# The scan of a four-operator image kernel: neighbour rows from a second, shifted copy of the state, in tiles of 32 columns

## The reference

```python
def _cell(prev_col, cur_col, weight_ih, bias_ih, weight_hh, bias_hh):
    C = cur_col.shape[-1]
    pad = jnp.pad(prev_col, ((0, 0), (1, 1), (0, 0)))
    x = jnp.concatenate([pad[:, :-2], pad[:, 1:-1], pad[:, 2:]], axis=-1)
    i_vals = jnp.einsum('bhk,ok->bho', x, weight_ih) + bias_ih
    h_vals = jnp.einsum('bhc,oc->bho', cur_col, weight_hh) + bias_hh
    r_i, z_i, n_i = jnp.split(i_vals, 3, axis=-1)
    r_h, z_h, n_h = jnp.split(h_vals, 3, axis=-1)
    r = jax.nn.sigmoid(r_i + r_h)
    z = jax.nn.sigmoid(z_i + z_h)
    n = jnp.tanh(n_i + r * n_h)
    return n * z + cur_col * (1.0 - z)
```

## Time and profile before

| | |
|---|---|
| Time, median of 3 runs | 601.97 us (601.34 to 603.91) |
| Span of the profiled execution | 600.5 us |
| PE busy | 551.9 us (92%), 7884 instructions |
| PE weight loads busy | 460.9 us (77%) |
| DVE busy | 469.2 us (78%), 1272 instructions |
| ACT busy | 394.4 us (66%), 897 instructions |
| POOL busy | 300.7 us (50%), 425 instructions |
| The chain that ended last | PE 39%, DVE 34%, ACT 15%, issue 9% of the span |

### The profile page before, as it was taken

The page is one execution under the profiler, slowest core; times in us unless marked ns, Lnnn a source line. Parts: engine busy times, 40 slices in busy tenths (PEclk is TensorE's granted clock), DMA queues, the critical chain, the costliest instruction groups (busy, mean ns, idle before and its releaser), DMA issues.

```text
span 600.5 us, 21552 instructions
## 1 busy us (share of the span) xinstructions
PE 551.9 (92%) x7884; PEld 460.9 (77%) x7884; DVE 469.2 (78%) x1272; ACT 394.4 (66%) x897; POOL 300.7 (50%) x425
## 2 busy tenths in 40 slices
PE   3999999699999999999999999988889897999996
PEld 2333333599998989899999999988477776899995
DVE  7778977377777777777778777888899999477876
ACT  3445889766666666666667966775468986766441
POOL 7665653156565655555565122035789799221000
PEclk9999999899999999999999999999999998999999
DMA  6900000011111111111111300001237675003324
GB/s 224 384 2 0 2 2 4 14 38 39 39 41 37 44 35 44 35 44 35 44 35 43 125 1 1 0 1 51 92 117 239 217 245 171 33 1 141 140 123 158
DMA packets 21282, 45.66 MB, mean 76 GB/s; under 512 B 5104, under 2 KB 15600, under 8 KB 20352
## 3 DMA queue, kind: packets, MB, share of 16 engines
q1 hardware_dynamic: 20160, 44.97, 23.2%
q10 hardware_dynamic: 672, 0.15, 0.1%
q0 software_dynamic: 416, 0.07, 0.1%
HBM read 28.53 MB, written 8.39 MB: 61 GB/s over the span
## 4 chain that ended last, share of the span: by engine, by line
PE 39%; DVE 34%; ACT 15%; issue 9%; DVEq 2%; DMA 1%; SPq 0%; POOL 0%; ACTq 0%; POOLq 0%
PE psum L645 8%; DVE work L326 5%; PE psum L755 5%; PE psum L894 5%; PE psum L910 5%; DVE spec L1343 5%; ACT spec L1001 5%; DVE spec L1335 5%; ACT spec L1009 5%; DVE spec L1338 4%; PE psum L813 4%; DVE small L1221 3%; PE psum L771 3%; PE psum L883 2%; PE psum L739 2%
## 5 line engine op out<-in xcount | busy, mean ns | idle before, releaser
L684 PE MATMUL psum<-spec,matrices 128*64 128x128 f32 x2016 | 154.7, 275 | 2.3 <-issue 1.5
L680 PE MATMUL psum<-spec,matrices 128*64 128x128 f32 x1512 | 132.4, 282 | 6.3 <-DVE spec L1343 3.7
L684 PEld LDWEIGHTS psum<-spec,matrices 128*64 128x64 f32 x2016 | 119.8, 138 | 3.1 <-issue 1.7
L522 POOL TENSOR_TENSOR spec<-spec 32x120 f32<-32x120 f32 x126 | 59.8, 475 | 88.5 <-DVE spec L1338 88.5
L680 PEld LDWEIGHTS psum<-spec,matrices 128*64 128x64 f32 x1512 | 85.3, 137 | 20.4 <-DVE spec L1343 8.6
L645 PE MATMUL psum<-spec,matrices 128*64 128x512 f32 x384 | 86.7, 609 | 1.0 <-ACT spec L935 1.0
L813 PE MATMUL psum<-work 128*32 128x128 f32 x2368 | 74.3, 278 | 14.0 <-ACT work L338 11.3
L813 PEld LDWEIGHTS psum<-work 128*32 128x32 f32 x2368 | 64.8, 111 | 23.3 <-issue 21.7
L326 DVE TENSOR_TENSOR work<-spec,psum 32x512 f32<-32x512 f32 x108 | 73.4, 680 | 3.8 <-PE psum L813 0.5
L497 POOL TENSOR_SCALAR spec<-image,small 32x960 f32<-32x960 f32 (+1 forms) x48 | 55.5, 1157 | 34.7 <-PE psum L645 22.3
L1001 ACT ACTIVATE spec<-spec 32x120 f32<-32x120 f32 x127 | 38.1, 300 | 48.6 <-DVE spec L1343 48.5
(11 more groups left out here) (153 smaller groups left out, 929.9 us busy)
## 6 DMA issues: line engine op xcount, KB each, us to landing
work<-w_dram SPq DMA_DIRECT2D x33, 512.0 KB, 3.6
spec<-work SPq DMA_DIRECT2D x124, 64.0 KB, 1.9
image<-x_dram SPq DMA_DIRECT2D x3, 2048.0 KB, 11.7
out_dram<-image SPq DMA_DIRECT2D x3, 2048.0 KB, 6.3
image<-x_dram SPq DMA_DIRECT2D x4, 512.0 KB, 6.0
work<-w_dram SPq DMA_DIRECT2D x1, 2048.0 KB, 7.6
out_dram<-image SPq DMA_DIRECT2D x4, 512.0 KB, 2.9
kept<-const_dram SPq DMA_DIRECT2D x1, 192.0 KB, 5.5
```

Of the source, the lines that this page charges most:

```text
L522: nc.gpsimd.tensor_tensor(lower_edge(h, parity), below(mix[h]), below(keep[h]), ALU.subtract).then_inc(lower_ready[h], 1)
L680: mm(psum[o, 4 * h + g, 0:HB], sv[:, g, o], state[h], start=True, stop=False)
L684: last = mm(psum[o, 4 * h + g, 0:HB], sv[:, 3 + g, o], e, start=starts, stop=True)
```

## The change

Each half gets another copy of the state, `straddle`, with 17 places of h4 instead of 16. ACT writes groups 2 and 3 (ROWS_23) at places 1 to 16, and GpSimd groups 0 and 1 (ROWS_01) at places 0 to 15; the two end places stay zero (a memset on DVE). Read from place 0, the copy holds what group 0 needs, and read from place 1, what group 3 needs. Groups 1 and 2 read the state itself. So the matmuls of a gate become four calls of 32 output columns (QUARTERS), and the weights of the wrapped neighbours go to sv[:, 0:3] instead of sv[:, 3:6]. The edge tiles now hold the current column and the ones alone; their matmuls (`from_column`, four calls each for r, z and h) start the sums. PE does them first, before it waits for either copy. The n gate has no such call; its bias is added in L1331, which becomes a scalar_tensor_tensor with the bias as a per-partition scalar. ACT does the update gate before the other half's copy. SP's loads wait for h_sum instead of z_sum. In DVE's half-step two pairs of waits change places.

```diff
@@ -157,6 +157,17 @@
         gr, gz, pre1, pre2, keep, mix = [[scan_buf() for _ in range(2)] for _ in range(6)]
         gn = [psum[:, 4 * h + 2, HB:2 * HB] for h in range(2)]
         bias_z = spec[:, off:off + 4 * C]
+        off += 4 * C
+        NBR = B // 2 * (H4 + 1)
+        straddle_both = spec[:, off:off + 2 * NBR]
+        straddle = [straddle_both[:, h * NBR:(h + 1) * NBR] for h in range(2)]
+        off += 2 * NBR
+        def straddled(h, q, first):
+            return straddle[h][q].rearrange("p (b h) -> p b h", h=H4 + 1)[:, :, first:first + H4]
         columns = work[:, 0:B * ROWS]
         stage = work[:, 0:4096]
...
@@ -410,8 +422,8 @@
                              scan_wi[:, :, C * (lo - hi + 1):C * (up - hi + 1)]).then_inc(scan_w_in, 16)
                 sp.dma_start(sv[C * hi:C * hi + C, 3:5, C * hi:C * hi + C], scan_wh[:, 0:2]).then_inc(scan_w_in, 16)
                 sp.dma_start(sv[C * hi:C * hi + C, 6, C * hi:C * hi + C], scan_wh[:, 2]).then_inc(scan_w_in, 16)
-            sp.dma_start(sv[P - C:P, 3:6, 0:C], scan_wi[:, :, 2 * C:3 * C]).then_inc(scan_w_in, 16)
-            sp.dma_start(sv[0:C, 3:6, P - C:P], scan_wi[:, :, 0:C]).then_inc(scan_w_in, 16)
+            sp.dma_start(sv[P - C:P, 0:3, 0:C], scan_wi[:, :, 2 * C:3 * C]).then_inc(scan_w_in, 16)
+            sp.dma_start(sv[0:C, 0:3, P - C:P], scan_wi[:, :, 0:C]).then_inc(scan_w_in, 16)
             sp.dma_start(kept[:, :], const_d[:, 0:sum(KEPT_COLS.values())]).then_inc(const_in, 16)
             sp.dma_start(forward_m, const_d[:, sum(KEPT_COLS.values()):]).then_inc(const_in, 16)
@@ -438,10 +450,10 @@
             with sp.Fori(0, (W - 4) // 2) as i:
                 for k in range(2):
                     for h in range(2):
-                        sp.wait_ge(z_sum[h], i * 2 + (k + 1))
+                        sp.wait_ge(h_sum[h], i * 2 + (k + 1))
                     current(i * 2 + (k + 3), (k + 1) % 2)
             for h in range(2):
-                sp.wait_ge(z_sum[h], W - 3)
+                sp.wait_ge(h_sum[h], W - 3)
             current(W - 1, 1)
             sp.wait_ge(state_ready[0], W)
@@ -505,35 +517,33 @@
                 normalise_parts(t // GB, t % GB)
             pool.wait_ge(norm_pool, 3 * B)
-            def lower_edge(h, parity):
-                return edges_of(h, parity)[1].rearrange("p (b h) -> p b h", h=H4)[0:C, :, 0:H4 - 1]
-
-            def below(buf):
-                return buf.rearrange("p (b h) -> p b h", h=H4)[0:C, :, 1:H4]
+            ROWS_01 = slice(0, P // 2)
             def add_state(h, w):
                 col = image[:, h * (B // 2 * ROWS):(h + 1) * (B // 2 * ROWS)] \
                     .rearrange("p (n w) -> p n w", w=W)[:, :, ds(w, 1)]
                 nc.gpsimd.tensor_tensor(col, col, state[h].unsqueeze(2), ALU.add).then_inc(added[h], 1)
-            def scan_step(h, w, parity):
+            def scan_step(h, w):
+                pool.wait_ge(mix_ready[h], w)
                 pool.wait_ge(keep_ready[h], w)
-                pool.wait_ge(mix_ready[h], w)
-                nc.gpsimd.tensor_tensor(lower_edge(h, parity), below(mix[h]), below(keep[h]),
-                                        ALU.subtract).then_inc(lower_ready[h], 1)
+                of = [t[h][ROWS_01].rearrange("p (b h) -> p b h", h=H4) for t in (mix, keep)]
+                nc.gpsimd.tensor_tensor(straddled(h, ROWS_01, 0), *of, ALU.subtract).then_inc(lower_ready[h], 1)
                 pool.wait_ge(state_ready[h], w + 1)
                 add_state(h, w)
+            pool.wait_ge(straddle_zeroed, 1)
             for h in range(2):
                 pool.wait_ge(state_ready[h], 1)
-                nc.gpsimd.tensor_copy(lower_edge(h, 1), below(state[h])).then_inc(lower_ready[h], 1)
+                nc.gpsimd.tensor_copy(straddled(h, ROWS_01, 0), state[h][ROWS_01].rearrange("p (b h) -> p b h", h=H4)
+                                      ).then_inc(lower_ready[h], 1)
                 add_state(h, 0)
             with pool.Fori(0, W // 2 - 1) as i:
                 for k in range(2):
                     for h in range(2):
-                        scan_step(h, i * 2 + (k + 1), k)
+                        scan_step(h, i * 2 + (k + 1))
             for h in range(2):
-                scan_step(h, W - 1, 0)
+                scan_step(h, W - 1)
             pool.wait_ge(t_done, 8)
@@ -671,33 +681,38 @@
             keep_warm(WARM_CONV_NORM, group_m)
-            HALVES = [slice(i * (P // 2), (i + 1) * (P // 2)) for i in range(2)]
-
-            def from_state(h, w, g):
-                if g == 0:
-                    pe.wait_ge(state_ready[h], w)
-                for o in HALVES:
-                    mm(psum[o, 4 * h + g, 0:HB], sv[:, g, o], state[h], start=True, stop=False)
-
-            def from_edges(h, g, parity, starts=False):
-                for o, e in zip(HALVES, edges_of(h, parity)):
-                    last = mm(psum[o, 4 * h + g, 0:HB], sv[:, 3 + g, o], e, start=starts, stop=True)
+            QUARTERS = [slice(C * hm, C * hm + C) for hm in range(HM)]
+            def from_state(h, g, starts=False):
+                moving = (straddled(h, slice(0, P), 0), state[h], state[h], straddled(h, slice(0, P), 1))
+                for hm in (1, 2, 0, 3):
+                    last = mm(psum[QUARTERS[hm], 4 * h + g, 0:HB], sv[:, g, QUARTERS[hm]], moving[hm],
+                              start=starts, stop=True)
                 return last
+            def from_column(h, g, parity, stops=False):
+                up, lo = edges_of(h, parity)
+                for q, e in zip(QUARTERS, (up, up, lo, lo)):
+                    last = mm(psum[q, 4 * h + g, 0:HB], sv[:, 3 + g, q], e, start=True, stop=stops)
+                return last
             def half_step(h, w, parity, nth):
-                from_state(h, w, 0)
-                from_state(h, w, 2)
                 if nth is None:
                     pe.wait_ge(cur_first[h], 32)
                 else:
                     pe.wait_ge(cur_in[parity], nth * 32)
+                    pe.wait_ge(r_gate[h], w - 1)
+                    pe.wait_ge(z_gate[h], w - 1)
+                    pe.wait_ge(reset_done[h], w - 1)
+                from_column(h, 0, parity)
+                from_column(h, 1, parity)
+                from_column(h, 3, parity, True).then_inc(h_sum[h], 1)
                 pe.wait_ge(sedge_ready[h], w)
                 pe.wait_ge(lower_ready[h], w)
-                from_edges(h, 0, parity).then_inc(r_sum[h], 1)
-                from_edges(h, 3, parity, True).then_inc(h_sum[h], 1)
-                from_edges(h, 2, parity).then_inc(n_sum[h], 1)
-                from_state(h, w, 1)
-                from_edges(h, 1, parity).then_inc(z_sum[h], 1)
+                from_state(h, 0).then_inc(r_sum[h], 1)
+                from_state(h, 2, True).then_inc(n_sum[h], 1)
+                from_state(h, 1).then_inc(z_sum[h], 1)
             pe.wait_ge(scan_w_in, 16 * 14)
             pe.wait_ge(bias_written, 2)
@@ -994,11 +1009,12 @@
                     bias=sh1[:, GB - 1:GB]).then_inc(columns_ready, 1)
-            def state_edges(h, w, parity):
+            ROWS_23 = slice(P // 2, P)
+            def state_edges(h, w):
                 act.wait_ge(state_ready[h], w + 1)
-                s = state[h].rearrange("p (b h) -> p b h", h=H4)
-                up = edges_of(h, parity)[0].rearrange("p (b h) -> p b h", h=H4)
-                a(up[P - C:P, :, 1:H4], s[P - C:P, :, 0:H4 - 1], ACT.Copy).then_inc(sedge_ready[h], 1)
+                a(straddled(h, ROWS_23, 1), state[h][ROWS_23].rearrange("p (b h) -> p b h", h=H4),
+                  ACT.Copy).then_inc(sedge_ready[h], 1)
             def reset_gate(h, w):
                 act.wait_ge(r_sum[h], w)
@@ -1012,23 +1028,23 @@
                 act.wait_ge(pre_ready[h], w)
                 a(gn[h], pre2[h], ACT.Tanh).then_inc(n_gate[h], 1)
-            def scan_step(w, parity):
+            def scan_step(w):
                 reset_gate(0, w)
-                state_edges(1, w - 1, parity)
                 update_gate(0, w)
+                state_edges(1, w - 1)
                 candidate(0, w)
                 reset_gate(1, w)
-                state_edges(0, w, 1 - parity)
                 update_gate(1, w)
+                state_edges(0, w)
                 candidate(1, w)
-            state_edges(0, 0, 1)
-            scan_step(1, 1)
-            scan_step(2, 0)
-            scan_step(3, 1)
+            act.wait_ge(straddle_zeroed, 1)
+            state_edges(0, 0)
+            for w in range(1, 4):
+                scan_step(w)
             with act.Fori(1, W // 4) as i:
                 for k in range(4):
-                    scan_step(i * 4 + k, k % 2)
+                    scan_step(i * 4 + k)
             act.wait_ge(added[0], W)
@@ -1293,6 +1309,7 @@
             for j in range(1, NG - 1):
                 conv_group(j, False, False)
             dve.wait_ge(small_in, 16 * 8)
+            v.memset(straddle_both, 0.0).then_inc(straddle_zeroed, 1)
```

(8 more changed lines are left out.)

1 line of the change is left out of this document (added).

## The result

The kernel after takes 597.5 us (median of 5 runs, 596.8 to 598.1); its time is 0.992 of before's, 95% interval 0.990 to 0.995. So it is faster by 4.4 us or 0.8%, and 597.5 is what I had forecast. The traces show that the scan's term was nearly right, and that two further terms, one wrong and one not foreseen, nearly cancel.

What follows compares the result with a forecast made beforehand. It took a 1.655 us scan half-step (state write, edge copy, update gate, DVE products) as the bound. Scan -5.6, start +1.0, memset +0.1 gave -4.5: span 600.5 to 596.0, plus 1.5 for the median, 597.5 us; range 592 to 603.

Steps and rivals of the forecast that it cites:

- the scan's term: Scan: 124 half-steps going from 1.655 to 1.61 us each, -5.6 us.
- The pace on PE and the four tiles side by side: PE: 48 32-column matmul instructions a half-step at 0.0267 us each, 1.28 us instead of 1.50; nothing taken for the gap.
- Rival 4: PE: quarters don't run side by side, or the clock halves; +115 us, time 717; chance 0.03.
- The circle of PE and ACT: Scan: new loop of edge copy, PE's state part, update gate, next edge copy; 1.59 us, without DVE's loop return.
- rival 2: PE and ACT's new circle needs 0.06 us more for a wait from standstill; time 602.5 or 600; chance 0.19.
- Rival 3: Same PE and ACT circle with PE's loop return or a GpSimd copy over 0.8 us; time 611; chance 0.10.
- DVE's circle: Scan: DVE's loop with the tanh takes 1.55 us, mean 1.61 with its loop return, and decides the half-step.
- The wait put first: DVE: with its wait for the preceding instruction first, L1331 starts 0.04 instead of 0.10 us after L1328's end.
- The pointer: DVE's L1331: the per-partition bias pointer raises it from 288 to 347 ns, 0.06 us more.
- rival 1: DVE's L1331: the bias pointer costs nothing, so the PE and ACT circle decides; time 593.2; chance 0.24.
- The chain's lines: Mid-scan chain of waits: would show DVE lines with the tanh.
- The start: Scan start: six column-part rounds ahead of the state part cost 0.6 to 1.3 us; taken as +1.0.

Runs made afterwards that it cites:

- e2: Changed kernel with DVE's two waits ahead of pre2 (the sum feeding the tanh) back in their old order; 606.7 us, 1.008 of before.
- e10: Changed kernel with GpSimd's addition of a state column to the image cut to 8 of its 128 elements per partition; 597.4 us, 0.993 of before.
- e7_waits_alone: Kernel before the change with only DVE's two pairs of waits exchanged; 601.3 us, 0.999 of before.
- e6: Changed kernel with PE's waits for the two copies moved ahead of the column part, so nothing is issued ahead; 690.0 us (one run).
- e8: Changed kernel with the n gate's bias summed by PE's column part and the z sum ahead of the n sum; 597.6 us, 0.995 of before.
- e11: Changed kernel with n gate's bias summed by PE, z sum ahead of n sum, and GpSimd's addition cut to 8 elements; 597.8 us, 0.994 of before.

## Why the prediction was right, and where it was not

*The pace on PE and the four tiles side by side: right.* L690's 24 instructions take 0.86 with the last one's 0.27, so 0.026 each, and the gap of one in 17 elements costs nothing that shows. Rival 4, with its 717 us, is out; the granted clock in mid-scan is 1.00.

*The circle of PE and ACT: right.* Summed 1.59. The edge copy L1016 comes at 251.96 and the next one at 253.55:

```profile
253.55 0.31 ACT L1016 ACTIVATE spec<-spec 64x128 f32<-64x128 f32 x1
```

That is 1.59, while DVE steps at 1.55; the 0.04 that it loses each time is given back at the loop return. PE, which reads two waits there, starts 0.05 after the copy's end: the 0.06 that rival 2 asked for isn't there. Rival 3 fell with it: no eighth step is longer, and GpSimd's copy takes 0.56, not over 0.8. GpSimd's copy ends 0.64 after mix's end (252.97 to 253.61), forecast 0.69, and is hidden.

*DVE's circle: right, link by link.* The wait put first: pre2 starts 0.03 after pre1's end, forecast 0.04, and e2 shows the old place to cost 0.08. The pointer: 351 ns, forecast 347; rival 1 is out. The return: 1.94 - 1.55 = 0.39. The mean is (5 x 1.55 + 1.94) / 6 = 1.615. The scan gave 5.1 us instead of 5.6 because I had rounded the mean to 1.61.

*The chain's lines: half right.* I named DVE's lines with the tanh. It is DVE's lines with the keep product, which I had taken at 292 ns and not looked at again, though its place moves into GpSimd's addition when the update gate no longer holds it. The size of this miss is 0.17 us in each step, and only luck of the margin kept it from costing: e10 shows the step the same with and without it.

*The start: wrong.* I took +1.0 for six rounds ahead of the state part. It is -0.6. Half 0's column part doesn't stand behind anything late: it was issued at 111.21, 4.7 us before the state part behind it (L690, 115.93). In half 1 PE waits for the DMA, before and after, and the step that failed is that I took its landing as given. The timelines of after, of before and of e7_waits_alone, which has before's PE and DMA code:

```profile
111.21 0.86 PE L697 MATMUL psum<-spec,matrices 128*32 128x128 f32 x24
115.57 0.23 DVE L1339 COPY spec<-work 128x128 f32<-128x128 f32 x1 [1.86 <-ACT work L295]
...
118.07 1.51 PE L697 MATMUL psum<-spec,matrices 128*32 128x128 f32 x24 [0.64 <-DMA spec<-work]
```

```profile
115.59 0.23 DVE L1322 COPY spec<-work 128x128 f32<-128x128 f32 x1 [1.87 <-ACT work L283]
```

```profile
114.74 0.23 DVE L1322 COPY spec<-work 128x128 f32<-128x128 f32 x1 [1.88 <-ACT work L283]
...
118.33 1.15 PEld L684 LDWEIGHTS psum<-spec,matrices 128*64 128x64 f32 x12 [0.34 <-DMA spec<-work]
```

From the copy of the second half's state to the second state write it is 7.24 in before (115.59 to 122.83) and 6.64 in after (115.57 to 122.21). PE's wait for the DMA parts it in two. From the copy to the end of this wait: 4.25 in before (119.84), 2.50 in after, 1.75 less. From there to the state write: 2.99 in before, 4.14 in after, 1.15 more; L697's six rounds stand in it with 1.25 (118.07 to L690's start at 119.32). So the rounds cost what I had priced, 0.6 to 1.3, and the earlier landing took back more than that. The memset's 0.1 doesn't show: the copy comes at the same time.

Why does the transfer land earlier? The DMA view of the 4.3 us from the copy on (packets, MB and share of a queue; KB and us from issue to landing of this transfer), first of before, then of after:

```profile
q8 instruction: 1, 0.02, 1.4%
spec<-work SPq DMA_DIRECT2D x2, 32.0 KB, 2.7
```

```profile
spec<-work SPq DMA_DIRECT2D x2, 32.0 KB, 1.8
```

In before a packet of instructions falls into this stretch, and in after none does. The same view of the other runs: e7 and e6 have the packet too, and 2.4 and 2.6 us to landing; the ten others, all with the column part ahead, have no packet and 1.8. In after and these ten PE's wait ends 2.49 to 2.51 after the copy. So the landing follows the kernel's code and isn't chance from one execution to the next. That the packet delays the transfer, and that the column part ahead moves the packet, is a pairing in 14 traces; no run moved the packet alone. e7's wait ends 3.59 after the copy, against 4.25 in before with the same PE and DMA code, so within such a pairing there is some 0.7 of play.

*What I had no term for.* The part behind the scan, whose code is the same, takes 1.15 us more in after's profile. The stretches with a half clock (0.50, which is 1.2 GHz) in the Fourier stage, of after and of before:

```profile
493.00:499.80 6.80, 5.85 (x112) 5.58 (x116) 6.49 (x11) 4.09 (x9) 6.42 (x8) 0.50 0.32 96
```

```profile
500.20:503.60 3.40, 3.40 (x72) 3.40 (x67) 3.24 (x6) 1.71 (x5) 3.25 (x5) 0.50 0.00 0
```

6.8 us of it against 3.4. Among the profiles of all the experiments this part took 271.7 to 274.6 us with 0 to 6.8 us of half clock and no edit in it, so 1.15 is within what it does by itself. The ten traces with 3.4 us of it took 272.4 to 272.8, the two with 6.8 (after, e8) 273.55 and 274.6, which goes with the clock; but the two with none took 271.7 and 273.0 (e7, e11), so that the clock is the whole cause isn't shown.

So -0.6 - 5.1 + 1.15 = -4.6, where I had written +1.0 - 5.6 + 0.1 = -4.5. The scan's term is right for the right reason. The start's lower value (1.7 below the forecast) was made up by this part and by 0.5 of the scan, so the agreement of the total to a tenth is chance.

## What to carry to other kernels

Where several circles of nearly one length run side by side, an edit has to be priced with all of them: the order of two waits was worth 0 or 9 us, and the update gate's place 6.5, depending on what else stood. Where an instruction has several waits, try the one first that is fulfilled last (it paid in the one pair tested here by itself); and find work (here the matmuls of the current column, worth 92 us) that needs nothing late and can stand ahead of a wait. After such a change read the loop returns: at a 1.55 us step, a return every ten steps instead of six gave another 4 us, and a body of 42 steps, whose return waited 2.8 us for instructions, took it all back.
